# Scan layers of a four-layer network: the loop over pass pairs written out in line

## What is computed

```python
seq = x.reshape(B, C, L).transpose(0, 2, 1)            # L = 1024 pixels in order
proj = seq @ W_proj.T + b_proj
x_in, delta, Bm, Cm = split(proj, [192, 384, 400])     # 192, 192, 16, 16
A = -exp(A_log); delta = softplus(delta + dt_bias)
# for each pixel t, 192 channels x 16 states:
h = exp(delta_t[..., None] * A) * h + (delta_t * x_t)[..., None] * B_t[:, None, :]
y_t = einsum('bdn,bn->bd', h, C_t)
out = (y + x_in * D) @ W_out.T + b_out
```

## Time and profile before

| what | value |
|---|---|
| median of 3 runs (4146.1 to 4152.93) | 4151.57 us |
| the profiled execution, its own time | 4148.75 us |
| its span, first to last instruction | 4146.9 us |
| convolution and attention, until the first scan of pass 0 | 1765.3 us of the span |
| the 32 passes, first scan to last scan | 2360.1 us |
| behind the last scan | 21.5 us |
| mean granted TensorE clock, share of full speed | 0.960 |

### The profile page before, as it was taken

How to read it: one execution, slowest core, us unless ns; L and a number is a source line. 1 busy time by engine, 2 the same in 40 slices (tenths; PEclk the granted TensorE clock), 3 DMA queues, 4 the chain that set the end, 5 groups by cost and what they waited for, 6 DMA issues and landing times.

```text
span 4146.9 us, 119527 instructions
## 1 busy us (share of the span) xinstructions
PE 3714.3 (90%) x49072; PEld 2319.4 (56%) x49072; DVE 3080.5 (74%) x3557; ACT 2021.2 (49%) x2675; POOL 2305.5 (56%) x877
## 2 busy tenths in 40 slices
PE   4996799889989998589999999999999999999998
PEld 4995566666666665345454454545555555455454
DVE  6563666666666775278878888888888888888887
ACT  2332254344444443355555555555655555555553
POOL 1111112112112111078888888888888888888887
PEclk9998799999999999699999999999999999999999
DMA  9724224223323322265645646656565564655644
GB/s 100 93 46 99 69 80 124 79 73 116 94 71 103 109 71 69 75 139 111 147 108 121 152 94 136 136 113 144 109 149 125 124 150 101 143 123 123 150 104 96
DMA packets 335727, 452.99 MB, mean 109 GB/s; under 512 B 53579, under 2 KB 207629, under 8 KB 335169
## 3 DMA queue, kind: packets, MB, share of 16 engines
q1 hardware_dynamic: 333840, 443.97, 48.5%
q10 hardware_dynamic: 1362, 1.39, 0.1%
HBM read 301.64 MB, written 94.37 MB: 95 GB/s over the span
## 4 chain that ended last, share of the span: by engine, by line
PE 29%; SPq 11%; DMA 10%; issue 5%; DVE 3%; ACT 0%; POOL 0%; DVEq 0%; POOLq 0%; ACTq 0%
PE ssm_u_ps L859 11%; PE ssm_y_ps L872 10%; DMA ssm_b_diag<-ssm_b_blocks 5%; SPq L768 4%; PE ssm_scratch L889 4%; SPq L747 3%; DVE ssm_h L1169 2%; PE ssm_u_ps L934 2%; DMA x_after_l<-ssm_x_res 1%; SPq L736 1%; DMA out<-ssm_x_res 1%; DMA ssm_b_blocks<-ssm_b_t 1%; SPq L728 1%; PE ssm_scratch L914 1%; SPq L717 1%
## 5 line engine op out<-in xcount | busy, mean ns | idle before, releaser
L1252 POOL TENSOR_TENSOR ssm_h<-ssm_h,ssm_c_rep 128x2048 f32<-128x2048 f32 x384 | 1751.4, 4571 | 127.4 <-DVE ssm_h L1169 127.4
L859 PEld LDWEIGHTS ssm_u_ps<-ssm_b_diag,ssm_dx_t 64*64 64x64 f32 x24576 | 754.6, 135 | 504.1 <-issue 502.6
L1169 DVE TENSOR_TENSOR_SCAN ssm_h<-ssm_decay,ssm_h,ssm_u_ps 128x512 f32<-128x512 f32 x768 | 934.5, 1258 | 125.6 <-PE ssm_u_ps L859 124.6
L859 PE MATMUL ssm_u_ps<-ssm_b_diag,ssm_dx_t 64*64 64x128 f32 x24576 | 934.1, 290 | 101.6 <-DMA ssm_b_diag<-ssm_b_blocks 57.9
L1008 ACT ACTIVATE ssm_decay<-ssm_delta_rep,ssm_a_neg 128x1024 f32<-128x1024 f32 x768 | 850.3, 1145 | 233.0 <-DVE ssm_h L1169 213.4
L1169 DVE TENSOR_TENSOR_SCAN ssm_h<-ssm_decay,ssm_u_ps 128x512 f32<-128x512 f32 x768 | 890.5, 1201 | 89.2 <-PE ssm_u_ps L859 61.1
L872 PE MATMUL ssm_y_ps<-ssm_h,ssm_state_sum 128*64 128x512 f32 x3072 | 770.6, 624 | 4.4 <-POOL ssm_h L1252 4.4
L1779 ACT ACTIVATE l_probs<-l_work 128x532 f32<-128x532 f32 (+1 forms) x384 | 217.3, 566 | 560.6 <-PE l_work L1633 554.0
L872 PEld LDWEIGHTS ssm_y_ps<-ssm_h,ssm_state_sum 128*64 128x64 f32 x3072 | 191.1, 139 | 316.2 <-issue 303.7
L1948 DVE RECIPROCAL l_den<-l_den 96x1024 f32<-96x1024 f32 x32 | 209.6, 6549 | 196.7 <-ACT l_den L1792 196.7
L2031 POOL TENSOR_TENSOR l_rstd<-l_var_eps,l_minus_half 96x2 f32<-96x2 f32 x16 | 11.1, 693 | 586.2 <-DVE l_var_eps L1868 586.2
(11 more groups left out here) (161 smaller groups left out, 5379.5 us busy)
## 6 DMA issues: line engine op xcount, KB each, us to landing
ssm_c_rep<-ssm_c_by_state SPq DMA_DIRECT2D x256, 512.0 KB, 10.4
ssm_delta_rep<-ssm_delta SPq DMA_DIRECT2D x384, 128.0 KB, 6.3
l_qk_parts<-l_qk SPq DMA_DIRECT2D x48, 768.0 KB, 4.7
ssm_b_diag<-ssm_b_blocks SPq DMA_DIRECT2D x512, 64.0 KB, 4.5
ssm_x<-x_after_l SPq DMA_DIRECT2D x32, 768.0 KB, 8.0
ssm_x_res<-x_after_l SPq DMA_DIRECT2D x64, 384.0 KB, 5.8
l_x<-x SPq DMA_DIRECT2D x64, 192.0 KB, 9.4
x_after_l<-l_x SPq DMA_DIRECT2D x64, 192.0 KB, 4.1
```

The costliest lines, as they stand in the source:

```text
L859: made = nc.tensor.matmul(u_ps[64 * par:64 * par + 64, ring("u", w), r, at:at + 128], dx_t[rows, db, 2 * win + k, 64 * g:64 * g + 64], of_ ...
L1169: nc.vector.tensor_tensor_scan(h[:, s % S_RING, npi, t], decay[:, 2 * (s % 2) + npi, t], u, start, ALU.mult, ALU.add).then_inc(scanned, 1)
L1252: nc.gpsimd.tensor_tensor(view, view, c_rep[:, 2 * q:2 * q + 2, :], ALU.mult).then_inc(c_applied, 1)
```

## The change

`schedule` no longer opens a loop on the engine: a Python loop writes the same calls out, trip after trip, with `it` a plain number. The layer argument is then worked out from `it` to the same value. Every instruction that does work, its order on its engine, and every DMA stay what they were; the sequencer's arithmetic goes, the waits hold constants, and the jump goes. `schedule` is called by all five engines, so this holds for each.

```diff
@@ -664,10 +664,9 @@
                     early(at(its, 0))
                     rest_and_next(its)
                 early(at(first, 0))
-                if last > first:
-                    with eng.Fori(first, last) as it:
-                        rest_and_next(it, layer)
-                        early(at(it + 1, 0, layer))
+                for it in range(first, last):
+                    rest_and_next(it, layer)
+                    early(at(it + 1, 0, layer))
                 rest_and_next(last)
             tail(at(2 * its - 1, 1))
```

## The result

The changed kernel takes 4083.41 us (median of 5 runs, 4075.95 to 4086.34) against 4151.57 before: a ratio of 0.9829, 95% interval 0.9805 to 0.9854, so 61 to 81 us faster. The forecast was 4088, range 4056 to 4110.

A forecast was written before the change was run, and what follows sets the result against it. PE was taken to set the pace, losing time at jumps back and diagonal waits. Gains of 39.6 (jumps), 8 (w3) and 16 us (the rest), 63.4 in all, gave 4088 us, range 4056 to 4110.

The forecast's parts named there:

- The jump: Window 10 of the ten passes with a jump back: PE's stop goes, 3.96 us each, 39.6 us in all.
- w3: Window 3 of a pass, where PE waits for the last diagonals: 6.05 to 5.68 us in 22 passes, 8 us.
- The other windows: All windows but w10 and w3: PE and DVE come sooner to their waits, 16 us, some 0.7 a pass.
- rival 3: In the 26 passes, sequencers stall fetching code run once, 3.96 us a stop: slower, 4191 with one each; chance 0.05.
- Rival 1: w3 nearly disappears as SP stays ahead: w3 at 4.2 to 5.0, gain 81 to 103 us, 4049 to 4070; chance 0.12.
- Rival 2: The jump isn't what costs in w10, the stop stays: gain 24 us, 4128; chance 0.08.
- What I said would show it: Profile signs: no projection issue wait over 1 us, w10 4.0 to 4.1, no pass above 73, diagonals about 3 us ahead.
- a sign of being wrong: Either w3's mean outside 5.0 to 6.46, or an engine's fixed-place stop for "issue" in passes without a jump.

## Why the prediction was right

**The jump.** 39.6 us were worked out from w10 beside w10 in line; 39.8 came. That it is the jump was read from four w10 without one, and two trips in place of six bear it out; that in the jump it is the code's fetch, the hint shows. That only PE's counts was an assumption; TensorE alone in line shows it.

**w3.** The mechanism held (SP's arithmetic delays the last diagonals), the size less so: 13.6 us for 8. Over 24 passes the diagonals go out 0.49 us sooner and land 0.24 us sooner (10.53 and 10.29 us into the pass), so half is given back, as was said; PE starts on window 4 0.35 us sooner (10.78 and 10.43), which is 8 us in 24 passes. The rest goes with the clock, which fell in 8 of these w3 in place of 12, at some 1.5 us a fall (6.46 beside 4.95). That part is luck: w3 takes 3.65 to 5.58 us where the clock holds and 6.38 to 7.11 where it falls, and the 109.3 and the 139.6 above, both with SP in line, say that 22 of them are few, and five fewer. The range had been made wide for this.

**The other windows.** 16 us were forecast (0.6 a pass over the 26, not the 0.7 given) and 10 came. The term took for granted that passes in line have no stops. They have, small ones; the timeline of PE in w6 of pass 5, changed kernel:

```profile
2144.41 0.69 PE L858 MATMUL ssm_u_ps<-ssm_b_diag,ssm_dx_t 64*64 64x128 f32 x11
2145.62 0.83 PE L858 MATMUL ssm_u_ps<-ssm_b_diag,ssm_dx_t 64*64 64x128 f32 x18 [0.53 <-issue]
```

There are five in the 26 passes, 0.4 to 1.4 us each, 3.4 in all, and nine of 0.4 to 0.8 us, 5.9 in all, in the same passes before, beside the jumps. PE waits for nothing there that the profile shows, and in each of the five the last packet of code had landed 1.2 to 1.5 us before PE went on. The missing 6 us lie in w6, w8 and w9, most of them in these five passes. This is rival 3's mechanism at a small price; that it is code coming late is read from the times, and no run takes it away. The errors of this term and of w3 cancel in the sum: 1868.8 for 1868.9 is luck.

**The rivals.** Rival 1 did not come: in line, w3 stays at 5.44 (4.97 with all loops in line, at the rival's edge), because SP's order and not its arithmetic makes most of it. Rival 2's 4128 fell with w10 at 4.02. The Trainium skill (Advanced Engine Details and Errata, Control Flow Timing) gives some 108 ns for a compare-and-branch; a jump of PE was measured here at 3.96 us of window, and the hint, which keeps the branch, takes all of it. Rival 3's stops are there: 5.9 us before, 3.4 in the changed kernel and 9.9 with all loops in line, whose scan layers are the same. So they are not shown to grow or to shrink, and two of them cost a clock fall as well.

**What I said would show it.** w10, the missing waits and the missing ALU_OP came. Wrong were three: six passes between 2 and 30 are above 73 us (pass 6 has 73.74); their lengths are not of two kinds but spread from 69.8 to 73.7; and SP's last diagonals are issued 1.7 to 3.0 us ahead of the pass, 2.46 on the mean, not about 3 everywhere. In line, too, SP is held by what it waits for earlier in `late`. By the letter, a sign of being wrong came as well, a stop for "issue" at a fixed place: DVE stands so ahead of w10 in each of passes 1 to 30. The waits view before (from pass 1 on), then in the changed kernel:

```profile
DVE ssm_h L1169 <- ACT ssm_decay L1008: 18.2, 24, 0.8
DVE ssm_h L1169 <- issue: 4.1, 6, 0.8
...
DVE ssm_h L1168 <- issue: 21.5, 30, 0.8
```

It is the idle time of before, which in the loop was put down to ACT; only the label changed. POOL's in w18 are of the same kind.

## What to carry to other kernels

Where part of a loop already stands in line, cut the trace at the passes and compare like windows: the written-out form is measured before it is written. A jump back of TensorE over a trip of some 4,000 instructions cost a stop here and most times a slow clock behind it; writing the trips out, or a hint of the jump's target, took it away, and only TensorE's jumps counted. A stall that the clock has a part in, such as w3, needs more than one profile: its sum differed by 10 us between two executions of the same scan layers. Then look at what stalls in every pass: here an exchange of two loads brought 72 us beside the 68 of the change.

## What the runs showed of the hardware

- A jump back of TensorE, with some 2,000 matmuls and as many weight loads in the trip, stops it for 2.2 to 2.9 us, and with the fall of the granted clock to 1.2 GHz that follows in eight of the ten the window is 3.96 us longer on the mean. With a branch hint on each trip it is 0 (ten w10: 40.65 us, in line 40.19).
- In straight code of many small matmuls (64 of them and their weight loads take some 2.2 us), too, TensorE stops for nothing that the profile shows: five times for 0.4 to 1.4 us in the changed kernel's 26 passes, with a DMA share of 0.86 to 1.06 in the 4 us ahead of them, and for up to 2.5 us in the other kernels (SyncE alone in line, pass 8).
- Behind a loop with the hint, DVE stood for 2.05 and 3.25 us in code without a jump, and for 2.06 and 5.44 us with the exchange; the cause is open.
